# Attention and routed feed-forward on one core: the causal mask of the stabilised scores by VectorE behind the exponential, not by TensorE ahead of it

## What is computed

```python
q = (x @ wq).reshape(b, s, 32, 32)
k = (x @ wk).reshape(b, s, 8, 32)      # each KV head serves 4 query heads
v = (x @ wv).reshape(b, s, 8, 32)
scores = einsum('bihd,bjhd->bhij', q, k) * 32 ** -0.5
scores = where(causal, scores, finfo.min)
attn = softmax(scores, axis=-1)
out = einsum('bhij,bjhd->bihd', attn, v) @ wo
```

## Time and profile before

| | us |
|---|---|
| runs: median of 3 (lowest, highest) | 3454.37 (3452.84, 3455.63) |
| the profiled execution | 3456.02 |
| its span in the trace | 3454.2 |
| DVE busy | 2002.2 |
| ACT busy | 1466.9 |
| attention: first and last mask product on PE start at | 547.0, 2565.0 |

### The profile page before, as it was taken

One profiled execution on the slowest core, in us unless ns is written; L12 is line 12 of the kernel. 1 busy time (PEld: TensorE's weight loads), 2 busy tenths in 40 slices (PEclk: granted clock), 3 DMA queues, 4 the chain that ended last, 5 costly groups with the idle time before them and its releaser, 6 DMA issues.

```text
span 3454.2 us, 61796 instructions
## 1 busy us (share of the span) xinstructions
PE 3406.8 (99%) x25202; PEld 2388.9 (69%) x25202; DVE 2002.2 (58%) x3620; ACT 1466.9 (42%) x1831; POOL 1748.0 (51%) x749
## 2 busy tenths in 40 slices
PE   9999999999999999999999999999999999999999
PEld 7888886565665666565666566566558888878887
DVE  3122117777667677777777767767746666642222
ACT  3111112555565565565565556556552333211111
POOL 0000003888988998898898898889550000000000
PEclk9999999999999999999999999999999999999999
DMA  6334343021111111111112111110047777754553
GB/s 219 116 121 123 115 137 94 24 53 50 35 43 50 38 38 51 51 31 47 50 33 53 50 35 43 50 40 10 26 113 234 231 234 229 219 203 169 174 176 132
DMA packets 248844, 340.60 MB, mean 99 GB/s; under 512 B 55680, under 2 KB 150400, under 8 KB 248576
## 3 DMA queue, kind: packets, MB, share of 16 engines
q1 hardware_dynamic: 248576, 336.87, 32.9%
HBM read 203.08 MB, written 133.17 MB: 97 GB/s over the span
## 4 chain that ended last, share of the span: by engine, by line
PE 64%; POOL 30%; issue 2%; DVE 2%; ACT 1%; DMA 0%; POOLq 0%; SPq 0%; ACTq 0%; DVEq 0%
POOL p_psums L714 27%; PE p_acc L42 13%; PE p_acc L44 12%; PE p_acc L43 12%; PE p_o L791 8%; PE p_qm L742 8%; PE p_km L784 5%; POOL p_psums L710 3%; DVE p_part_max L903 1%; PE p_km L777 1%; PE p_ag_ps L1220 1%; PE p_km L779 1%; PE p_acc L1209 1%; ACT p_probs L867 1%; PE p_qm L746 1%
## 5 line engine op out<-in xcount | busy, mean ns | idle before, releaser
L903 DVE TENSOR_REDUCE p_part_max<-p_qm 128x1 f32<-128x512 f32 (+3 forms) x2240 | 1399.7, 670 | 556.2 <-PE p_qm L742 347.1
L714 POOL TENSOR_TENSOR p_psums<-p_psums,p_probs 128x1024 f32<-128x1024 f32 x620 | 1480.7, 2388 | 92.1 <-ACT p_probs L867 2.1
L867 ACT ACTIVATE p_probs<-p_km 128x1024 f32<-128x1024 f32 x896 | 887.8, 1023 | 459.0 <-PE p_km L784 448.6
L742 PE MATMUL p_qm<-p_k_st,p_q_st 96*128 96x512 f32 (+3 forms) x2560 | 908.6, 416 | 10.5 <-ACT p_neg_max L849 4.6
L742 PEld LDWEIGHTS p_qm<-p_k_st,p_q_st 96*128 96x128 f32 x2560 | 474.0, 191 | 255.8 <-issue 93.4
L784 PE MATMUL p_km<-p_q_st,p_k_st 97*128 97x512 f32 x1792 | 601.7, 417 | 10.6 <-ACT p_probs L867 8.3
L791 PE MATMUL p_o<-p_probs,p_v 128*32 128x256 f32 (+1 forms) x9216 | 566.8, 372 | 0.0
L791 PEld LDWEIGHTS p_o<-p_probs,p_v 128*32 128x32 f32 x9216 | 271.1, 110 | 222.5 <-issue 51.5
L784 PEld LDWEIGHTS p_km<-p_q_st,p_k_st 97*128 97x128 f32 x1792 | 310.8, 192 | 98.9 <-ACT p_probs L867 61.2
L710 POOL TENSOR_TENSOR p_psums<-p_probs 128x1024 f32<-128x1024 f32 x110 | 261.9, 2381 | 188.3 <-ACT p_probs L867 188.3
L699 POOL MEMSET p_k_st<- 1x2048 f32 x2 | 3.6, 1805 | 508.4 <-PE p_acc L44 508.4
(11 more groups left out here) (160 smaller groups left out, 3982.5 us busy)
## 6 DMA issues: line engine op xcount, KB each, us to landing
p_q_st<-q_hi SPq DMA_DIRECT2D x128, 256.0 KB, 4.6
p_x_raw<-in_xT SPq DMA_DIRECT2D x64, 256.0 KB, 3.4
q_hi<-p_out_hi SPq DMA_DIRECT2D x64, 256.0 KB, 2.0
q_lo<-p_out_lo SPq DMA_DIRECT2D x64, 256.0 KB, 2.3
p_q_st<-q_lo SPq DMA_DIRECT2D x64, 256.0 KB, 4.4
attended_T<-p_o_raw SPq DMA_DIRECT2D x128, 128.0 KB
p_a_raw<-attended_T SPq DMA_DIRECT2D x32, 512.0 KB, 9.7
p_recip<-reciprocals SPq DMA_DIRECT2D x128, 128.0 KB, 7.0
```

Of the source, the lines that this page charges most:

```text
L714: pool.tensor_tensor(sums[:, :, :], sums[:, :, :], probs[(n * NS + s) % PB][:, :, :], ALU.add).then_inc(added, 1)
L742: last = pe.matmul(bank[:, x * keys:(x + 1) * keys], q_st[par][0:ROWS, c, h + x, sub * P:(sub + 1) * P], k_st[par][0:ROWS, j * CK:j * CK + ...
L867: act.activation(tile[:, :, :].rearrange("p h q -> p (h q)"), km[s % 2][:, :, :].rearrange("p a b -> p (a b)"), ACT.Exp, scale=SCALE).then ...
L903: dve.reduce_max(part_max[c][:, h:h + heads, sub, j], qm[bank_of(i)][:, 0:item_width(i)].rearrange("p (h k) -> p h k", h=heads), AX.X).the ...
```

## The change

The product with `mask_k` and its tile are taken out. The exponential is taken of the uncut scores. A new tile `limit` holds 3e38 where a key is allowed and 0 where it is cut, and DVE takes the element-wise minimum of the diagonal block of `probs` and `limit`, in place: for each diagonal step one instruction on 128 x (4 x 128) f32 (`limit_diagonal`), 16 in a pass. DVE does both minima of a chunk at the end of its last slot, behind that slot's maxima and ahead of those of the next. A new semaphore `limited` is waited for by PE ahead of the values of a chunk's last slot, and by POOL ahead of those adds that take a diagonal step (t = 2 of chunk 1 and t = 4 of chunk 2). Step t = 2c is now computed like any other; step t = 2c + 1 keeps its half.

```diff
             self.ident = tmp("p2_ident", [P, P])
-            self.ident_bf, self.mask_q, self.mask_k = (tmp(f"p2_{n}", [P, P], BF16) for n in ("ident_bf", "mask_q", "mask_k"))
+            self.ident_bf, self.mask_q = (tmp(f"p2_{n}", [P, P], BF16) for n in ("ident_bf", "mask_q"))
+            self.limit = tmp("p2_limit", [P, P])
...
-            pool.memset(mask_k[:, :], 0.0).then_inc(ident_done, 1)
+            pool.memset(limit[:, :], LIMIT).then_inc(ident_done, 1)
...
-            pool.affine_select(out=mask_k[:, :], in_=mask_k[:, :], compare_op=ALU.is_ge, fill=NEG,
+            pool.affine_select(out=limit[:, :], in_=limit[:, :], compare_op=ALU.is_ge, fill=0.0,
                                base=0, pattern=[[1, P]], channel_multiplier=-1).then_inc(consts_done, 1)
...
                         pool.wait_ge(exp_done, n * NS + s + 1)
+                        if t >= 2 * c:
+                            pool.wait_ge(limited, n * 2 * NC + t + 1)
                         if t == 1:
...
-                if t >= 2 * c:
-                    first = t - 2 * c
-                    for x in range(1, first - 1, -1):
-                        four = pair[:, x, :].rearrange("p (h q) -> p h q", h=REP)
-                        last = pe.matmul(four, keys, q_st[par][0:ROWS + 1, c // 2, :, q0 + x * P:q0 + (x + 1) * P],
-                                         start=True, stop=x > first)
-                    last = pe.matmul(four, ident_bf[:, :], mask_k[:, :].unsqueeze(1).to_broadcast([P, REP, P]),
-                                     start=False, stop=True)
+                if t == 2 * c + 1:
+                    last = pe.matmul(pair[:, 1, :].rearrange("p (h q) -> p h q", h=REP), keys,
+                                     q_st[par][0:ROWS + 1, c // 2, :, q0 + P:q0 + CQ], start=True, stop=True)
                 else:
...
                 pe.wait_ge(exp_done, n * NS + steps[-1] + 1)
+                if STEPS[steps[-1]][1] == 2 * c + 1:
+                    pe.wait_ge(limited, n * 2 * NC + 2 * c + 2)
...
-                if t >= 2 * c:
-                    first = t - 2 * c
-                    act.activation(tile[:, :, first * P:CQ].rearrange("p h (x q) -> p x h q", q=P),
-                                   km[s % 2][:, first:2, :].rearrange("p x (h q) -> p x h q", h=REP),
+                if t == 2 * c + 1:
+                    act.activation(tile[:, :, P:CQ], km[s % 2][:, 1, :].rearrange("p (h q) -> p h q", h=REP),
                                    ACT.Exp, scale=SCALE).then_inc(exp_done, 1)
...
         def vector(dve):
+            def limit_diagonal(n, s):
+
+                c, t = STEPS[s]
+                x = t - 2 * c
+                diagonal = probs[(n * NS + s) % PB][:, :, x * P:(x + 1) * P]
+                dve.wait_ge(exp_done, n * NS + s + 1)
+                dve.tensor_tensor(diagonal, diagonal, limit[:, :].unsqueeze(1).to_broadcast([P, REP, P]), ALU.min
+                                  ).then_inc(limited, 1)
+
             def group(n, placed):
-                for items in placed:
-                    for ahead, i in items:
-                        max_item(dve, n + ahead, i)
+                for _, steps in SLOTS:
+                    for s in steps:
+                        for ahead, i in placed[s]:
+                            max_item(dve, n + ahead, i)
+                    for s in steps:
+                        c, t = STEPS[s]
+                        if t >= 2 * c:
+                            limit_diagonal(n, s)
```

More of the change, by code:

```diff
@@ L509, in attend @@
         rest_of_q = sb("p2_rest_of_q", [P, S // P * HD + BANK * REP], F32)
[L510 to L511 removed]
+        ident, ident_bf, mask_q, limit, ones = (opening.ident, opening.ident_bf, opening.mask_q, opening.limit,
+                                                opening.ones)
         part_max, row_max, neg_max = opening.part_max, opening.row_max, opening.neg_max
```

4 lines of the change are left out of this document (2 added, 2 removed).

## The result

The changed kernel took 3704.55 us (median of 4 runs, 3701.43 to 3709.49) against 3454.17 for the kernel before beside it: a ratio of 1.0721, 95% interval 1.0708 to 1.0734. It is slower, as forecast, but by 250 us where 105 were forecast, beyond the upper end of the range (3628). The profiled execution took 3707.18 us, its span is 3705.4.

What follows compares the result with a forecast made beforehand. PE and POOL were taken as nearly balanced, with PE's new stalls setting the pass. 10.5 + 0.7 - 3.8 - 0.45 = +7.0 us a pass, +105 over fifteen, -2 in the last: 3456 + 103 = 3559 us, range 3493 to 3628.

Steps and rivals of the forecast that it cites:

- What bounds the kernel: In the attention, PE and POOL balance to half a microsecond from chunk 4 to 7; PE's savings need POOL's too.
- Removed from PE, -3.8 us: In a middle pass, 16 mask matmuls leave PE at 0.235 us each, saving 3.8 us.
- Late ends, +10.5 us: After chunks 3 to 7, two minima alternate with POOL's adds, 4.8 us; PE stalls 2.3 us net each, 10.5 a pass.
- the 2.2 that I named: Sign in the profile after: the 256 minima on DVE have a mean near 2.2 us, far over 0.68.
- Early ends, +0.7: After chunks 0 to 2, minima mostly fit DVE's gaps or POOL waits for them; cost 0.7 us a pass.
- the wait for POOL, -0.45: At the end of chunk 7, PE's 0.45 us wait for POOL goes, since PE now comes later.
- POOL becomes the bound: Rival: DVE keeps the lock for both minima, late ends cost 0.5 us, POOL's 127.6 us sets the pass; 3502 us, chance 0.2.
- DVE hardly notices POOL: Rival: a minimum takes 0.68 us beside a running add and PE gets its time back; 3431 us, chance 0.05.
- the stalls are longer: Rival: the first minimum also meets a fresh add, 3.7 us at five late ends, +14 a pass; 3670 us, chance 0.1.
- The last pass, -2: In the last pass, with only 25 POOL adds, perhaps two stalls remain against 3.8 us of saving: -2 us.

Runs made afterwards that it cites:

- x3_no_mask: The changed kernel without the minima and the waits for them, so with neither mask products nor minima: 3458.93 us, ratio 1.0013.
- x11_no_mask_fewer_adds: The changed kernel without minima or mask products, and with 43 POOL adds a pass instead of 47: 3447.41 us, ratio 0.9975.
- x12_before_fewer_adds: The kernel before, with its mask products, and four POOL adds a pass fewer: 3475.15 us, ratio 1.0057.
- x4_both: The changed kernel with the mask products on PE kept beside the minima, and limit held as bf16: 3711.46 us, ratio 1.0745.
- x8_filler: The changed kernel with 40 useless PE products more a pass, placed where PE would stall after chunks 3 to 7: 3621.55 us, ratio 1.0476.
- x7_early_only: The changed kernel with minima for chunks 0 to 2 only, mask products for chunks 3 to 7, limit in bf16: 3456.53 us, ratio 1.0007.
- x1_split_early: The changed kernel with the last pass's split of wo done in two parts between chunks, not behind the last minima: 3683.23 us, ratio 1.0667.
- x9_mask_in_psum: The changed kernel with the minimum taken on the scores in PSUM before the exponential, and the split of wo moved earlier: 3486.61 us, ratio 1.0085.

## Why the prediction was right, and why its size was wrong

**What bounds the kernel: right as far as it was tested.** PE's saving is worth nothing without POOL's: in `x3_no_mask` PE waits for POOL's sum. But taking POOL out of the way (`x11_no_mask_fewer_adds`) left the pass as long (123.93 us for 123.97), with the products with ones of four more steps on PE.

**Removed from PE, -3.8 us: over-sized.** The sixteen products were worth 1.6 us (`x12_before_fewer_adds` against `x11_no_mask_fewer_adds`), and beside the minima 0.1 to 0.2 (`x4_both`). The row gave their price on a busy PE, and I didn't subtract the waits that take it up. Error: at least +2.2 us a pass, 33 in fifteen.

**Late ends, +10.5 us: right in mechanism, somewhat over-sized.** The alternation taken from the earlier trace rows is there. Three runs show that the price hangs on what the instruction reads and writes in SBUF and on the length of the add: a small result (0.675 us), an input and the result in PSUM (0.69), shorter adds (1.199). The prediction named the two SBUF inputs as the cause; that isn't separated from the result in SBUF, and the cast of its own rows has one such input. A late pair takes 2.9 to 4.3 us, 3.9 in the mean of the five shown, where I had 4.8: the second minimum takes its whole add as priced, the first one meets the end of an add rather than its middle, and after chunk 5 there is only one add. So a pass has four stalls of 1.4 to 2.3 us (one of 3.6 in fourteen passes) and not five of 2.8. PE's idle time grew by 7.7 us a pass where the prediction's stalls, net of the waits given back, were 10.5 + 0.7 - 0.45 = 10.75. The upper bound by `x8_filler`, 9.1 + 1.6 (products) = 10.7 us, is no confirmation of that figure. The mean of all minima (1.40 us) is below the 2.2 that I named, partly because six of sixteen run undisturbed.

**Early ends, +0.7, and the wait for POOL, -0.45: right.** 1.28 us for a pair, POOL's adds 1.32 and 0.85 us late, `x7_early_only` the same as before. Rival "POOL becomes the bound" is refuted: the adds do overtake, and POOL has 0% of the chain. "DVE hardly notices POOL" as well: minima beside adds take up to 2.9 us.

**The clock, in no term: the largest miss.** I counted a stall as time in which PE does nothing, and took its speed afterwards for granted; the earlier trace rows show a clock of 1.00. It is at least 6.1 us a pass, 92 us in fifteen, and up to 9.6, 144 us. It is also why the total came close to the rival "the stalls are longer" (3670) without its cause: the stalls are shorter than forecast. The trace of the kernel before had the sign: in its last pass the clock falls three times, the first time with no idle time of PE over 0.74 us in the 10 us ahead of it.

```profile
2508.90:2512.30 3.40, 3.40 (x34) 1.38 (x32) 3.40 (x2) 1.45 (x2) 3.26 (x2) 0.50 0.94 317
```

The Trainium skill (TensorE: Matmul & The Clock Gate, "A second HAM failure mode: psum-queue depth-cycling") tells of a kernel in which short idle times of PE between groups of matmuls, coming often enough, made its clock oscillate; the rows here agree, 0.50 behind stalls of 1.96 to 2.09 us.

**The last pass, -2: right inside (-3.0), missed behind it.** I saw that the split of wo runs there, took its prices from it, and didn't ask what becomes of it when two minima of chunk 7 stand ahead of it in DVE's queue. That is +25 us; `x1_split_early` takes 21.3 off the whole by the order alone.

Summed with the lower bound of the clock and the late ends as forecast: 103 + 33 (products) + 92 (clock) + 25 (queue at the end) = 253; the span grew by 251.2. Part of that agreement is luck, since two of the terms are bounds. Counted from PE's side, a pass has 7.7 us more of idle time, up to 9.6 of lost clock and 1.6 less of work: 15.7, for 15.2 measured. Either way the clock, which I had at nothing, is the largest part of what the forecast lacks.

**Open.** Why the clock falls after some stalls of about 2 us and not after others, in `x3_no_mask` after three of fourteen nearly equal waits, was not settled. The 6.1 us are a lower bound, since the filler has its own cost; the 9.6 us of work missed by the clock rows are the upper one. Whether the second SBUF input or the result in SBUF makes the minimum wait needs an operation with just one of them, which was not run. Why `x9_mask_in_psum` loses 7.7 us up to the end of the first pass and 7.5 in the last, where ACT waits for its minima, was not tried further.

## What to carry to other kernels

Moving work from an engine that is full to one with 40% of free time is priced by what the operation shares with a third engine: an element-wise operation with two inputs and its result in SBUF waits for whole GpSimd adds, and the same operation with one input and the result in PSUM doesn't. Behind forecast stalls of TensorE (here of 1.4 to 2.3 us, four in 140) put a second term, the work that follows at half clock, and look in the trace of before whether its clock ever falls behind waits. Ask for the last pass too what is queued behind the new wait. And before pricing a saved product at its back-to-back time, look whether it lies beside a wait that stays: here it was worth 0.10 us of 0.235, and next to nothing beside the new stalls.
